# A graph kernel's message stage: the products of values and softmax weights go from VectorE to GpSimd

## The chip, the cores and the metric

The kernel runs on one core of a Trainium2 chip. The metric is the device time of one execution in microseconds (us), here the median of three runs. The profile is of one further execution.

## The reference

Four graph networks run one after the other on the same graph of 3125 nodes with 128 features and 50000 edges, sorted by destination. After each, the result is added to its input and normalised. The fourth is a graph transformer of two layers, and only the last step of its layer matters here. Cut to that:

```
m = vT[src, :, etype]                     # E x 8 heads x 16: the values of each edge
att = edge_softmax(a, dst, n)             # E x 8: a weight for each edge and head
msg = (m * att[:, :, None]).reshape(-1, H * HS)
hag = jax.ops.segment_sum(msg, dst, num_segments=n)
h = jax.nn.silu(typed_linear(hag, ntype, Wa))
```

All of it is float32.

## The kernel before

The edges lie in 416 tiles (`STEPS`) of 128. Each tile belongs to one block of 128 destination nodes. A segment sum over a tile is a matmul: a one-hot matrix, 128 edges by 128 destinations of the block, is the stationary operand, the messages of the 128 edges are the moving one, and the result is added to the block's columns in PSUM (`accf`). Four tiles are a quad, of which there are 104 (`ALL_QUADS`), and four quads are a trip. The first of the 26 trips is written out, the other 25 are a hardware loop (`trips`, L78).

`message_phase` (L1584) runs once in each of the transformer's two layers, after the scores and their softmax, and with a barrier before and behind it. Its instructions stand in four queues, and each queue is executed in its order:

- SyncE loads the values of a quad (256 KB, L1593) into one of four slots of `vals`. From the second trip on it waits until the product that used the slot is made (L1592).
- VectorE runs the helper `onehots` (L330): for each quad a wait that TensorE has finished the quad two before (`quad_done`, L339, as the one-hots have two buffers), the one-hots of four tiles in one comparison (128x512, L341), which signals `onehot_ready`, and then `weigh` (L1599): a wait for the values (`ring_in`, L1600) and the product of the values with the weights, 128x512, into one of two buffers of `msgs` (L1602), which signals `mixed`. Both `msgs` and `vals` are parts of the tile `arena`.
- TensorE clears the banks (`fill_rows`, L386), then for each quad loads one register with four packed block numbers (`quad_blocks`, L368), unpacks them (L370), waits for `mixed` (L1616) and makes four matmuls (L1619). Each is a float32 matmul, which the trace shows as two passes with a weight load each, so eight passes in a quad. The last one signals `quad_done`. TensorE does not wait for `onehot_ready`: VectorE makes the one-hot before the product.
- GpSimd and ScalarE have nothing to do in the stage.

In other stages GpSimd gathers rows by indirect DMA and copies columns (L1243, L1246). The aggregation stages (L531 to L547) have a TensorE loop of the same form that waits for two semaphores at the start of a quad: `onehot_ready` (L537) and the gathered rows (L540).

Of the kernel before, what the change touches and what calls it, by code (L numbers as in the profile page):

```python
# [5 lines left out]
ALU = mybir.AluOpType  # L6
# [4 lines left out]
ds = bass.ds  # L11

P = 128
# [7 lines left out]
U = 16  # L21
HALF = U // 2
QUADS = U // 4
# [15 lines left out]
HEADS = 8  # L39
HS = H // HEADS  # L40
# [34 lines left out]
def trips(eng, body, n=TRIPS):  # L75

    body(0, True)
    with eng.Fori(1, n) as i:  # L78
        body(i, False)
# [7 lines left out]
def build(nc, A, out):  # L87
    ctx = ExitStack()
    with ctx:
# [3 lines left out]
        def signal(name):  # L93
            return Signal(ctx.enter_context(nc.semaphore(name)))
# [65 lines left out]
        onehot_ready = signal("onehot_ready")  # L160
        compared = signal("compared")
        quad_done = signal("quad_done")
# [4 lines left out]
        mixed = signal("mixed")  # L167
# [4 lines left out]
        ring_in = [signal(f"ring_in{u}") for u in range(HALF)]  # L172
# [158 lines left out]
        def onehots(dve, weight, after=None):  # L331


            def body(i, first):
                for q in range(QUADS):
                    n = i * QUADS + q
                    j = i * U + 4 * q
                    if not (first and q < 2):
                        dve.wait_ge(quad_done.sem, quad_done.at(n - 1))  # L339
                    o = onehot[:, 4 * (q % 2):4 * (q % 2) + 4, :]  # L340
                    is_dst = dve.tensor_tensor(o, iota_row[:, :].unsqueeze(1).to_broadcast([P, 4, P]),  # L341
                                               dl_s[:, ds(j, 4)].unsqueeze(2).to_broadcast([P, 4, P]), ALU.is_equal)
                    if weight is not None:
                        is_dst.then_inc(compared.sem, 1)
                        dve.wait_ge(compared.sem, compared.at(n + 1))
                        is_dst = dve.tensor_tensor(o, o, weight[:, ds(j, 4)].unsqueeze(2).to_broadcast([P, 4, P]), ALU.mult)  # L346
                    is_dst.then_inc(onehot_ready.sem, 1)
                    if after is not None:
                        after(i, q, first)
            trips(dve, body)  # L350
            if weight is not None:
                compared.base += ALL_QUADS
# [13 lines left out]
        def quad_blocks(pe, n):  # L366

            four = nc.values_load(blk4_i[0:1, ds(n, 1)], engines=(pe.engine,), min_val=0, max_val=32 ** 4 - 1,  # L368
                                  skip_runtime_bounds_check_because="block numbers by construction")
            return [nc.snap((four >> (5 * c)) & 31, engines=(pe.engine,), min_val=0, max_val=NB - 1) for c in range(4)]  # L370

        def quad_pass_over():
            onehot_ready.base += ALL_QUADS
            quad_done.base += ALL_QUADS
# [6 lines left out]
        def fill_rows(pe, row):  # L381

            for k in range(BANKS):
                a, b, blocks = span(k)
                if row is None:
                    pe.matmul(accf[:, a:b], ident[:, :], zeros[:, 0:b - a], start=True, stop=False, skip_group_check=True)  # L386
                else:
                    pe.matmul(accf[:, a:b].rearrange("p (b f) -> p b f", f=H), ones[0:1, :],
                              row.unsqueeze(1).to_broadcast([1, len(blocks), H]), start=True, stop=False, skip_group_check=True)
# [576 lines left out]
        if STAGE >= 4:  # L966
# [13 lines left out]
            score = arena[:, 3200:3200 + STEPS * HEADS].rearrange("p (s h) -> p s h", h=HEADS)  # L980
# [19 lines left out]
            vals = arena[:, 7600:7600 + U * H].rearrange("p (r f) -> p r f", r=U)  # L1000
            msgs = arena[:, 9648:9648 + HALF * H].rearrange("p (r f) -> p r f", r=HALF)
# [582 lines left out]
            def message_phase():  # L1584

                with nc.Block() as block:
                    @block.sync
                    def _(sp):
                        def body(i, first):
                            for q in range(QUADS):  # L1590
                                if not first:
                                    sp.wait_ge(mixed.sem, mixed.at(i * QUADS + q - 3))  # L1592
                                sp.dma_start(vals[:, 4 * q:4 * q + 4, :],  # L1593
                                             values[ds(i * U + 4 * q, 4), :, :].rearrange("a e f -> e a f")).then_inc(ring_in[q].sem, 16)
                        trips(sp, body)

                    @block.vector
                    def _(dve):
                        def weigh(i, q, first):  # L1599
                            dve.wait_ge(ring_in[q].sem, ring_in[q].at(16 * (i + 1)))  # L1600
                            r = 4 * (q % 2)
                            dve.tensor_tensor(msgs[:, r:r + 4, :].rearrange("p s (h o) -> p (s h) o", o=HS),  # L1602
                                              vals[:, 4 * q:4 * q + 4, :].rearrange("p s (h o) -> p (s h) o", o=HS),
                                              score[:, ds(i * U + 4 * q, 4), :].rearrange("p s h -> p (s h)").unsqueeze(2).to_broadcast([P, 4 * HEADS, HS]),
                                              ALU.mult).then_inc(mixed.sem, 1)
                        onehots(dve, None, weigh)

                    @block.tensor
                    def _(pe):
                        fill_rows(pe, None)  # L1610

                        def body(i, first):
                            for q in range(QUADS):
                                blocks = quad_blocks(pe, i * QUADS + q)

                                pe.wait_ge(mixed.sem, mixed.at(i * QUADS + q + 1))  # L1616
                                for c, b in enumerate(blocks):
                                    o = onehot[:, 4 * (q % 2) + c, :]
                                    mm = pe.matmul(accf[:, ds(b * P, P)], o, msgs[:, 4 * (q % 2) + c, :],  # L1619
                                                   start=False, stop=False, skip_group_check=True)  # L1620
                                mm.then_inc(quad_done.sem, 1)
                        trips(pe, body)
                quad_pass_over()
                mixed.base += ALL_QUADS
                for s in ring_in[0:QUADS]:
                    s.base += 16 * TRIPS
# [138 lines left out]
```

## Time and profile before

| | |
|---|---|
| median of three runs | 7607.94 us (7606.06 to 7610.19) |
| the profiled execution | 7653.93 us |
| its span in the profile | 7652.2 us |
| TensorE busy, of the span | 4183.2 us (55%) |
| VectorE busy | 2372.6 us (31%) |
| GpSimd busy | 3561.7 us (47%) |
| the two message stages | 205.1 us each |

In the profile PE is TensorE's matmuls, PEld its weight loads, DVE is VectorE, ACT is ScalarE, POOL is GpSimd, SP is SyncE. A q behind an engine (PEldq) means its instruction queue: register, branch and semaphore instructions, which are not counted as busy. What ended an engine's idle time stands behind an arrow; "issue" means that the profile shows nothing that it waited for. PEclk is the granted clock of TensorE, where 1.0 is full speed.

### The profile page before, as it was taken

What the parts mean: (1) busy time and instruction counts of PE and PEld (TensorE: products, weight loads), DVE (VectorE), ACT (ScalarE), POOL (GpSimd) and SP (SyncE); (2) the same over time, 40 slices, a digit from 0 to 9 for tenths busy, and PEclk for the clock granted to TensorE, in tenths of its full rate; (3) what the DMA queues carried; (4) which work ended last, traced back from release to release, by engine and by line L of the source; (5) the groups of instructions that cost most, each with busy time, mean ns of one, the idle gap of its engine ahead of it and who ended that gap; (6) DMA issues with size and microseconds to landing.
All of it is one profiled execution on the core that took longest, in us unless ns stands there. A gap on an engine that the chain in (4) does not pass through costs nothing. (4 is left out here: it accounts for less than half of the span.)

```text
span 7652.2 us, 76944 instructions
## 1 busy us (share of the span) xinstructions
PE 4183.2 (55%) x15969; PEld 3034.6 (40%) x15970; DVE 2372.6 (31%) x3036; ACT 928.1 (12%) x1558; POOL 3561.7 (47%) x3650
## 2 busy tenths in 40 slices
PE   3566577667646666345443269544353299444352
PEld 2565445445435554233332134333242144333242
DVE  5222322322232223111111333233562233333753
ACT  0000222222211111000000012100000022000001
POOL 2675566366626663665676210466302201666111
PEclk8555676766765556556655589756586699656685
DMA  1111333233313332112211257544232367444241
GB/s 41 45 45 38 80 98 98 71 92 98 99 46 87 88 87 100 46 45 80 68 46 46 74 196 306 190 132 131 80 112 81 108 276 287 130 132 130 62 118 45
DMA packets 619686, 791.03 MB, mean 103 GB/s; under 512 B 89114, under 2 KB 508944, under 8 KB 594008
## 3 DMA queue, kind: packets, MB, share of 16 engines
q1 hardware_dynamic: 491800, 497.65, 19.4%
q0 software_dynamic: 127808, 292.52, 14.3%
q8 instruction: 27, 0.44, 0.0%
q14 instruction: 51, 0.42, 0.0%
HBM read 433.80 MB, written 356.02 MB: 103 GB/s over the span
## 5 line engine op out<-in xcount | busy, mean ns | idle before, releaser
L363 POOL DMA_INDIRECT G<-table,idx_s x3328 | 3329.2, 1000 | 2200.6 <-issue 934.9
L544 PE MATMUL ps<-G,onehot 128*128 128x128 f32 x4160 | 1169.0, 415 | 685.5 <-issue 506.2
L341 DVE TENSOR_TENSOR onehot<-iota_row,dl_s 128x512 f32<-128x512 f32 x1040 | 716.8, 690 | 1879.2 <-remote 1028.3
L544 PEld LDWEIGHTS ps<-G,onehot 128*128 128x128 f32 x4160 | 886.5, 286 | 905.8 <-issue 901.6
L1402 PE MATMUL ps<-arena 128*128 x1664 | 394.6, 395 | 505.0 <-issue 460.7
L1402 PEld LDWEIGHTS ps<-arena 128*128 128x128 f32 x1664 | 327.9, 283 | 581.3 <-issue 580.1
L1351 DVE TENSOR_TENSOR arena<-G,ps 128x512 f32<-128x512 f32 x208 | 142.7, 686 | 868.6 <-remote 533.6
L1262 PE MATMUL ps<-arena,G 128*128 128x512 f32 x800 | 379.1, 596 | 35.1 <-DVE arena L1294 35.1
L1305 DVE COPY arena<-ps 128x1024 f32<-128x1024 f32 x200 | 244.9, 1225 | 448.2 <-PE ps L1270 448.2
L1270 PE MATMUL ps<-arena,G 128*128 128x512 f32 x800 | 375.9, 592 | 0.0
L714 DVE TENSOR_TENSOR arena<-arena 128x256 f32<-128x256 f32 x208 | 88.6, 426 | 882.6 <-issue 529.8
L1097 POOL DMA_INDIRECT sorted_x<-Hn,pos_i x50 | 48.0, 961 | 653.6 <-POOLq L1652 639.0
L1619 PE MATMUL ps<-arena,onehot 128*128 128x128 f32 x1664 | 263.2, 310 | 135.3 <-issue 119.3
L635 PE MATMUL ps<-arena 128*128 128x256 f32 x416 | 204.8, 586 | 239.7 <-ACT arena L683 152.6
L859 PEld LDWEIGHTS ps<-ones,onehot 128*128 128x128 f32 x832 | 221.9, 327 | 265.6 <-issue 265.5
L543 PEld LDWEIGHTS ps<-ones,onehot 128*128 128x128 f32 x832 | 223.4, 328 | 252.0 <-issue 251.8
L859 PE MATMUL ps<-ones,onehot 128*128 128x1 f32 x832 | 191.7, 300 | 238.3 <-issue 127.7
L861 PE MATMUL ps<-onehot,arena 128*128 128x128 f32 x832 | 320.8, 489 | 0.0
L543 PE MATMUL ps<-ones,onehot 128*128 128x1 f32 x832 | 182.4, 289 | 240.5 <-DVE onehot L346 217.5
L1391 PE MATMUL ps<-ident,onehot 128*128 128x128 f32 x832 | 197.0, 383 | 197.0 <-issue 128.7
L1243 POOL COPY G<-HF 128x128 f32 (+1 forms) x50 | 14.8, 295 | 611.8 <-PE ps L1262 598.0
L1619 PEld LDWEIGHTS ps<-arena,onehot 128*128 128x128 f32 x1664 | 226.9, 212 | 171.4 <-issue 169.9
(287 smaller groups left out, 4715.0 us busy)
## 6 DMA issues: line engine op xcount, KB each, us to landing
table<-arena SPq DMA_DIRECT2D x200, 1024.0 KB
G<-table,idx_s POOLq DMA_INDIRECT x3328
values<-G SPq DMA_DIRECT2D x208, 256.0 KB
arena<-values SPq DMA_DIRECT2D x208, 256.0 KB
arena<-edge_times SPq DMA_DIRECT2D x208, 128.0 KB
edge_part<-arena SPq DMA_DIRECT2D x208, 128.0 KB
arena<-edge_part SPq DMA_DIRECT2D x416, 64.0 KB
table<-arena SPq DMA_DIRECT2D x50, 512.0 KB
```

Source lines behind the costliest of these rows:

```text
L341: is_dst = dve.tensor_tensor(o, iota_row[:, :].unsqueeze(1).to_broadcast([P, 4, P]), dl_s[:, ds(j, 4)].unsqueeze(2).to_broadcast([P, 4, P] ...
L363: pool.indirect_dma_start(G[:, j % U, 0:width], None, tab, bass.IndirectOffsetOnAxis(ap=idx_s[:, j:j + 1], axis=0)).then_inc(gathered[j % ...
L543: pe.matmul(misc[:, ds(b, 1)], o, ones[:, 0:1], start=False, stop=False, skip_group_check=True)
L544: mm = pe.matmul(accf[:, ds(b * P, P)], o, G[:, u, 0:H], start=False, stop=False, skip_group_check=True)
L635: pe.matmul(self.half_b, self.We2, self.hid[:, r, :], start=True, stop=True, skip_group_check=True).then_inc(turned.sem, 1)
L859: pe.matmul(misc[:, ds(b, 1)], o, ones[:, 0:1], start=False, stop=False, skip_group_check=True)
L861: mm = pe.matmul(accf[:, ds(b * P, P)], relu_h[:, u % HALF, :], o, start=False, stop=False, skip_group_check=True)
L1262: mm = pe.matmul(ps[:, s + c, :], node_cols[:, 0, :], block_k[:, 8 * q + 4 * c:8 * q + 4 * c + 4, :].rearrange("p t c -> p (t c)"), start= ...
L1270: mm = pe.matmul(ps[:, s + 2 + c, :], node_cols[:, 1, :], block_v[:, 8 * q + 4 * c:8 * q + 4 * c + 4, :].rearrange("p t c -> p (t c)"), st ...
L1305: dve.tensor_copy(rows32[:, q, :, H:2 * H], ps[:, 4 * (q % 2) + 2:4 * (q % 2) + 4, :].rearrange("p a (t f) -> p (a t) f", f=H)).then_inc(c ...
L1402: mm = pe.matmul(ps[:, 4 + q, c * P:(c + 1) * P], onehotT[:, q % 2, c * P:(c + 1) * P], Qn_flat[:, ds(b * P, P)], start=True, stop=True)
L1619: mm = pe.matmul(accf[:, ds(b * P, P)], o, msgs[:, 4 * (q % 2) + c, :], start=False, stop=False, skip_group_check=True)
```

## The change

VectorE keeps only the one-hots. GpSimd gets a program in the stage: for each quad it waits until TensorE has finished the quad two before, then for the values, and makes the product. TensorE waits for `onehot_ready` and for `mixed`, since the two now come from different engines. SyncE's program is as before.

```diff
                     @block.vector
                     def _(dve):
-                        def weigh(i, q, first):
-                            dve.wait_ge(ring_in[q].sem, ring_in[q].at(16 * (i + 1)))
-                            r = 4 * (q % 2)
-                            dve.tensor_tensor(msgs[:, r:r + 4, :].rearrange("p s (h o) -> p (s h) o", o=HS),
-                                              vals[:, 4 * q:4 * q + 4, :].rearrange("p s (h o) -> p (s h) o", o=HS),
-                                              score[:, ds(i * U + 4 * q, 4), :].rearrange("p s h -> p (s h)").unsqueeze(2).to_broadcast([P, 4 * HEADS, HS]),
-                                              ALU.mult).then_inc(mixed.sem, 1)
-                        onehots(dve, None, weigh)
+                        onehots(dve, None)
+
+                    @block.gpsimd
+                    def _(pool):
+                        def body(i, first):
+                            for q in range(QUADS):
+                                if not (first and q < 2):
+                                    pool.wait_ge(quad_done.sem, quad_done.at(i * QUADS + q - 1))
+                                pool.wait_ge(ring_in[q].sem, ring_in[q].at(16 * (i + 1)))
+                                r = 4 * (q % 2)
+                                pool.tensor_tensor(msgs[:, r:r + 4, :].rearrange("p s (h o) -> p (s h) o", o=HS),
+                                                   vals[:, 4 * q:4 * q + 4, :].rearrange("p s (h o) -> p (s h) o", o=HS),
+                                                   score[:, ds(i * U + 4 * q, 4), :].rearrange("p s h -> p (s h)").unsqueeze(2).to_broadcast([P, 4 * HEADS, HS]),
+                                                   ALU.mult).then_inc(mixed.sem, 1)
+                        trips(pool, body)
 
                     @block.tensor
                     def _(pe):
@@ -1613,6 +1620,7 @@
                             for q in range(QUADS):
                                 blocks = quad_blocks(pe, i * QUADS + q)
 
+                                pe.wait_ge(onehot_ready.sem, onehot_ready.at(i * QUADS + q + 1))
                                 pe.wait_ge(mixed.sem, mixed.at(i * QUADS + q + 1))
                                 for c, b in enumerate(blocks):
```

## Rows read from the trace of the kernel before

**Rows 1.** The page: busy us of each engine, share of the span.
```profile
PE 4183.2 (55%) x15969; PEld 3034.6 (40%) x15970; DVE 2372.6 (31%) x3036; ACT 928.1 (12%) x1558; POOL 3561.7 (47%) x3650
```

**Rows 2.** First message stage: length, PE, PEld, DVE, ACT, POOL busy, PEclk, DMA.
```profile
5584.20:5789.30 205.10, 136.87 (x846) 115.69 (x846) 133.67 (x208) 0.01 (x1) 0.00 (x0) 0.93 0.46 133
```

**Rows 3.** Timeline of a quiet trip: start us, length, engine, line.
```profile
5766.76 1.15 PE L1619 MATMUL ps<-arena,onehot 128*128 128x128 f32 x8 [1.09 <-issue]
5768.60 1.15 PE L1619 MATMUL ps<-arena,onehot 128*128 128x128 f32 x8 [0.68 <-issue]
5769.90 0.69 DVE L341 TENSOR_TENSOR onehot<-iota_row,dl_s 128x512 f32<-128x512 f32 x1 [0.54 <-PE ps L1619]
5770.43 1.15 PE L1619 MATMUL ps<-arena,onehot 128*128 128x128 f32 x8 [0.68 <-issue]
5770.51 0.68 DVE L1602 TENSOR_TENSOR arena<-arena 128x512 f32<-128x512 f32 x1
5772.25 1.15 PE L1619 MATMUL ps<-arena,onehot 128*128 128x128 f32 x8 [0.67 <-issue]
5774.56 0.71 PE L1619 MATMUL ps<-arena,onehot 128*128 128x128 f32 x4 [1.15 <-issue]
```

**Rows 4.** Lines L368, L370, L78 in TensorE's queue, first stage; ns min/median/max.
```profile
L368 PEldq TENSOR_LOAD <-blk_i x104: 296/301/331, 5584.3 to 5786.5; - x104
L370 PEldq ALU_OP  x416: 32/32/36, 5584.7 to 5787.4; - x139
L370 PEldq FUSED_REGOPS  x412: 40/58/68, 5584.8 to 5787.5; - x138
L78 PEldq COMPARE_BRANCH  x25: 76/208/218, 5602.1 to 5788.3; - x25
```

**Rows 5.** The matmul line L1619, whole span, with its waits.
```profile
L1619 PEldq FUSED_REGOPS  x832: 46/49/52, 5587.6 to 7422.6; - x167
  issue: 289.1, 333
  DVE arena L1602: 15.6, 19
```

**Rows 6.** The product line L1602, whole span.
```profile
L1602 DVE TENSOR_TENSOR arena<-arena x208: 680/684/693, 5586.9 to 7420.6; 128x512 f32<-128x512 f32 x104
```

**Rows 7.** Timeline where the clock is low.
```profile
5743.43 4.82 PE L1619 MATMUL ps<-arena,onehot 128*128 128x128 f32 x24 [1.12 <-issue]
5745.53 0.69 DVE L341 TENSOR_TENSOR onehot<-iota_row,dl_s 128x512 f32<-128x512 f32 x1 [1.78 <-PE ps L1619]
5748.92 1.15 PE L1619 MATMUL ps<-arena,onehot 128*128 128x128 f32 x8 [0.67 <-DVE arena L1602]
```

**Rows 8.** The wait line L540 of the aggregation stages, TensorE's queue.
```profile
L540 PEldq EVENT_SEMAPHORE  x395: 2/51/711, 130.0 to 4253.4; - x198
L540 PEldq FUSED_REGOPS  x75: 4/52/707, 160.0 to 4232.1; - x75
```

**Rows 9.** GpSimd's copies, line view.
```profile
L1246 POOL COPY G<-Hn x50: 295/296/301, 4482.7 to 6464.6; 128x128 f32 x48, 128x128 f32<-128x128 f32 x2
L1193 POOL COPY arena<-arena x2: 2848/2848/2849, 4472.8 to 6107.7; 128x3200 f32<-128x3200 f32 x2
```

**Rows 10.** Timeline at 4278, and VectorE's same operation at L488.
```profile
4278.06 2.85 POOL L1633 COPY Lx<-Xn 128x3200 f32<-128x3200 f32 x1 [28.69 <-ACTq L1630]
4278.07 3.28 DVE L1639 SCALAR_TENSOR_TENSOR arena<-src_s,t_s 128x416 f32<-128x416 f32 x1 [0.53 <-PEq L429]
L488 DVE SCALAR_TENSOR_TENSOR arena<-src_s,t_s x2: 591/592/592, 2933.9 to 3596.4; 128x416 f32<-128x416 f32 x2
```

**Rows 11.** Timeline at the start of the first message stage.
```profile
5584.20 14.79 SPq L1593 DMA_DIRECT2D arena<-values  x11
5586.85 0.69 DVE L1602 TENSOR_TENSOR arena<-arena 128x512 f32<-128x512 f32 x1 [1.92 <-DMA arena<-values]
5589.69 1.95 PE L1619 MATMUL ps<-arena,onehot 128*128 128x128 f32 x16
```

## The prediction

> **What bounds the kernel now.** I read the page first. The span is 7652.2 us and no engine is near full: TensorE is busy 55% of it, GpSimd 47%, VectorE 31% [rows 1]. That average says nothing of this change, which touches one stage, run twice: the message stage of the graph transformer. The stretches view has a row for each of the two runs, of which one is shown and the other is like it within 0.3%: 205.1 us each, 410.2 us together, 5.4% of the span. In them VectorE works 134 us, TensorE 137 us, GpSimd nothing at all [rows 2]. So no engine's arithmetic fills the stage, and the question is what sets the pace of a quad (four tiles, 104 quads in each run).
>
> The timeline of a quiet piece answers it [rows 3]. TensorE starts a quad at 5768.60, 5770.43 and 5772.25: 1.83 us each. Its eight passes take 1.15, then it idles 0.68, "issue", which names no releaser. Once in four quads the gap is 1.15. From 5766.76 to 5774.56, one trip of four quads, it is 7.80 us, or 1.95 a quad. VectorE starts the one-hot at 5769.90, that is 0.15 after the passes of 5768.60 end (5769.75), and the product at 5770.51; this is for the quad after the next (two buffers), so its end at 5771.19 is 1.06 us before TensorE uses it at 5772.25. The product is not what TensorE waits for.
>
> The line views of TensorE's own queue say what fills the gap [rows 4]. A quad needs: the load of the packed block numbers (one record of 0.30), four ALU_OP and four FUSED_REGOPS to unpack them (L370; 416 and 412 for 104 quads), a FUSED_REGOPS ahead of the load, and four more at the matmuls (832 in 208 quads, in [rows 5]). That is 14 steps in 1.83 us, through one in-order sequencer. Without the load's 0.30 it leaves 1.53 for 13 steps, 0.12 a step, though a record itself takes only 0.03 to 0.06. In the quad that begins a trip, three loop steps (L78) stand where one did; the gap is 0.47 longer (1.15 against 0.68), of which the branch's record is 0.21. The stage's pace is therefore TensorE's instruction stream. The waits view of the matmul line agrees: 289.1 us "issue" against 15.6 us put down to VectorE's product, in 19 places [rows 5].
>
> **The change, part by part.** *Removed from VectorE:* 208 products of 0.684 us [rows 6], with their waits. They lie beside TensorE's stream and the last of them is ready early, so I cost this at nothing. What it could return is the 15.6 us of 19 gaps [rows 5]. But such a gap is as long as an ordinary one: the one at 5748.92 is 0.67, put down to the product, where "issue" gaps are 0.68 [rows 3, 7]. On average the 19 are 0.82, so 19 x 0.14 = 2.7 us could come back at the most. I take 0.
>
> *Added to TensorE:* one more wait in each quad, 208 in all. Before, the wait for the product covered the one-hot too, as VectorE made it first; its wait is carried by the first address step. In the aggregation stages, where TensorE waits for two semaphores at the start of a quad, the first of them is a record of its own at L540, EVENT_SEMAPHORE or FUSED_REGOPS, of median 51 and 52 ns [rows 8]. So I expect one more step in the stream that sets the pace. Its price lies between the bare record, 0.05 (nothing, if it should fit into a gap that I don't see, but an in-order stream leaves none), and the mean step, 0.12. The mean includes long ones (the branch of memory and register steps), so I take 0.105: 208 x 0.105 = **+22 us**. The ends are +10 and +25. Behind this wait stand the eight weight loads and passes of the quad, and behind those the release of both buffers; everything in the stage shifts with it.
>
> *Added to GpSimd:* 208 products of 128x512 from two SBUF operands. No such operation is in the trace. The nearest rows are its copies, one input: 0.295 us for 128 elements, 2.848 for 3200 [rows 9]. That is 0.83 ns an element and 0.19 fixed, so 0.61 us for 512, the least it can be. If it reads its two inputs in turn, 1.04. If reads and the write all come in turn, 1.47. I take 1.25, between the last two, as the product must at least read twice what a copy reads. Rough bounds for the sum are 1.04 and 1.47.
>
> *Contention.* The one-hot and the product are now released together, by the same quad's passes. The trace has one case of such a pair. At 4278.06 GpSimd begins a copy of 2.85 us; 0.01 us later VectorE begins an operation with two SBUF inputs that takes 3.28 us, while the same operation on the same shape takes 0.592 elsewhere, and GpSimd's copy isn't slowed [rows 10]. VectorE stood still for 2.69 of the copy's 2.85. So they exclude each other, and the later one waits. The Trainium skill ("SBUF — State Buffer", Who interferes with whom) says this for a VectorE instruction with two SBUF inputs against a GpSimd one that reads SBUF; the trace agrees in its one case. By that rule the one-hot would always fall on one side of the product; without it they would overlap and nothing would be added.
>
> VectorE needs 0.15 from release to start, and GpSimd has two waits to pass before its instruction, so I let the one-hot go first: 0.15, then 0.61 (the spacing of VectorE's instructions, 5769.90 to 5770.51 [rows 3]), then 1.25, then some 0.2 until TensorE starts: 2.2 us after the release. TensorE's own stream gives 5772.25 - 5769.75 = 2.50 today and 2.50 + 2 x 0.105 = 2.71 with the new wait. So it is hidden with 0.5 to spare. Throughput: 0.61 + 1.25 + 0.1 for the two hand-overs = 1.96 a quad, against 1.95 + 0.105 = 2.05. Hidden too, by 0.1 only.
>
> Where the clock is low it isn't hidden. The granted clock is 0.93 over the stage [rows 2]: taking 1.2 against 2.4 GHz, 14% of it, some 29 quads. There TensorE starts at 5743.43 and releases VectorE only at 5745.53 - 0.15 = 5745.38, so 1.95 after its start instead of 1.15 [rows 7]. Two quads on is 3.66 + 0.21 = 3.87 after the start, 1.92 after the release; the chain needs 2.2. That is 0.28 late per two quads, 29 x 0.14 = 4 us; trips' long quads take a part of it back: **+3 us**.
>
> *The queues.* SyncE loads the values four quads ahead and waits for the product of the quad whose slot it refills. The product ends 0.6 us later than now (2.0 against 1.4 after the release), and three quads are 6 us; a load takes 2.65 us from issue to use (the first quad's: issued at 5584.20, product at 5586.85 [rows 11]). Hidden. At the stage's start TensorE clears its banks and starts the first quad at 5589.69; the second product would be made by 5586.85 + 2 x 1.25 = 5589.35 [rows 11]. Hidden. GpSimd's next work, after the stage, starts when the stage ends.
>
> **Sum.** The profiled execution took 7653.93 us (span 7652.2), 0.6% over the median of 7607.94. Its sum is 7653.93 + 22 + 3 = 7679; on the median, 7607.94 + 25 = **7633 us**, 0.33% slower.
>
> **Rivals.**
> *GpSimd sets the pace.* If the product is 1.47 and shares nothing with the one-hot, a quad is 0.61 + 1.47 + 0.1 = 2.18, 0.13 over 2.05: 208 x 0.13 = 27 us more, 7660. If the hand-overs cost the full 0.15 each and the one-hot its 0.69, it is 2.46, 85 us more, 7718, the far end. For it: the margin of my forecast is 0.1 us in a quad, and GpSimd's price is not in the trace. Against it: 0.14 of the copy's record didn't hold VectorE up, so records overlap at their ends. The Trainium skill ("GPSIMD Engine Reference", Performance versus the Vector engine) gives 4497 ns for a two-input addition of 2048 elements; no row here shows one. With the copies' fixed part that is an estimate of 1.27 us for 512, by which the sum would stay at 7633.
>
> *The wait costs nothing or half.* If the step is only its record, 208 x 0.05 = 10 us, 7618 with nothing added for the slow pieces; if it is swallowed, 7608. Against it: the 0.68 gap is itself made of nothing but such steps, each of which costs twice its record.
>
> *Faster.* The product leaves VectorE, which then has its one-hot ready at once, and the 15.6 us put down to the product in 19 gaps come back in full: 7592. It decides if these gaps were truly waits and the new wait is hidden under the load of the block numbers. Against it: their length is the length of any gap, and the first condition returns 2.7 us at most.
>
> **How the numbers follow.** Forecast (7620 to 7645) 0.60; GpSimd at the pace (7645 to 7718) 0.25; cheap or swallowed wait (7604 to 7620) 0.11; faster 0.04. The range leaves out the fastest case, half of the cheap one and the far end of the slow one: 7614 to 7675. A change of 0.2% is 15 us, about what a measurement of this kernel can tell. Slower by more: all of the first two but its low corner, 0.84. Within it 0.13. Faster by more 0.03.
>
> **What would show it.** In the profile after, the wait step appears in TensorE's queue at its line, 104 times a stage, and a quiet trip grows from 7.80 to 8.2 us with the gaps still "issue". Each stage takes 205.1 + 12 = 217 us. GpSimd has 208 products of about 1.25 us, or records up to 1.9 where the one-hot holds it up, and some one-hots of VectorE are far longer than 0.69. I am wrong if the TensorE gaps are put down to GpSimd in most quads (then the product is the pace), or if a quiet trip stays at 7.80 (then the wait is free).

## The result, and the profile after

Ten runs of each kernel, side by side: 7630.2 us median after (7624.29 to 7634.59), 7609.25 us before (7601.94 to 7615.32). The ratio is 1.0028, its 95% interval 1.0018 to 1.0038: 21 us slower, where 25 were forecast (7633). The profiled execution took 7634.59 us, close to its median, while that of the kernel before (7653.93) was 45 us above its own. So the two spans must not be subtracted; the message stages can be.

The stretches view of the changed kernel, its two message stages (length, then PE, PEld, DVE, ACT, POOL busy, PEclk, DMA share, GB/s):

```profile
5541.60:5758.40 216.80, 147.24 (x846) 124.50 (x846) 75.42 (x104) 0.00 (x0) 155.73 (x104) 0.88 0.43 126
7184.60:7401.70 217.10, 146.68 (x846) 124.01 (x846) 74.64 (x104) 0.00 (x0) 155.70 (x104) 0.88 0.43 126
```

Against 205.1 us each [rows 2] that is 11.7 and 12.0 longer, 23.7 together: the whole change of time, within what the runs can tell. VectorE's work has fallen from 134 to 75 us and nothing came of it.

The timeline of one quiet trip after, the answer to [rows 3]:

```profile
5641.45 0.69 DVE L341 TENSOR_TENSOR onehot<-iota_row,dl_s 128x512 f32<-128x512 f32 x1 [1.24 <-PE ps L1627]
5641.60 1.45 POOL L1609 TENSOR_TENSOR arena<-arena 128x512 f32<-128x512 f32 x1 [0.48 <-PE ps L1627]
...
5644.48 1.15 PE L1627 MATMUL ps<-arena,onehot 128*128 128x128 f32 x8 [1.27 <-DVE onehot L341]
5646.41 1.15 PE L1627 MATMUL ps<-arena,onehot 128*128 128x128 f32 x8 [0.78 <-issue]
5648.34 1.15 PE L1627 MATMUL ps<-arena,onehot 128*128 128x128 f32 x8 [0.77 <-issue]
5650.25 1.15 PE L1627 MATMUL ps<-arena,onehot 128*128 128x128 f32 x8 [0.75 <-issue]
```

The next quad starts at 5652.67, so the trip takes 8.19 us; it was 7.80. The passes take 1.15 as before, and each gap has grown by 0.08 to 0.12. TensorE's queue has what makes it so, the new wait as a record of its own, 104 times a stage. It is only 36 ns long in 200 of the 208 cases (the forecast expected 51 or 52), but the next step of the queue starts 0.097 us after it (median in the trace):

```profile
L1624 PEldq ALU_OP  x200: 36/36/36, 5553.7 to 7400.1; - x100
L1624 PEldq EVENT_SEMAPHORE  x8: 51/51/51, 5545.4 to 7194.7; - x8
```

GpSimd's product, and what waited for it (first line: ns min/median/max):

```profile
L1609 POOL TENSOR_TENSOR arena<-arena x208: 1055/1502/1562, 5544.3 to 7398.2; 128x512 f32<-128x512 f32 x104
...
  PE ps L1627: 18.4, 29
```

The shortest is 1.055 us; with a one-hot beside it, it is 1.45 to 1.56.

### The profile page after: what moved, and what is told of

Its sections match the earlier page's. It is cut to its first block and busy times, and to the rows that moved or that the text cites. A ratio compares the mean times of both kernels' runs of the same rounds, so it can differ in the third digit from the quotient of the medians.

```text
span 7632.8 us, 77558 instructions
## 1 busy us (share of the span) xinstructions
PE 4239.0 (56%) x15969; PEld 3069.8 (40%) x15970; DVE 2256.0 (30%) x2828; ACT 928.5 (12%) x1558; POOL 3869.6 (51%) x3858
## 5 line engine op out<-in xcount | busy, mean ns | idle before, releaser
L1609 POOL TENSOR_TENSOR arena<-arena 128x512 f32<-128x512 f32 x208 | 311.4, 1502 | 343.4 <-DMA arena<-values 230.5
L1627 PE MATMUL ps<-arena,onehot 128*128 128x128 f32 x1664 | 283.0, 324 | 139.5 <-issue 64.7
L1627 PEld LDWEIGHTS ps<-arena,onehot 128*128 128x128 f32 x1664 | 243.5, 225 | 178.8 <-issue 177.1
L543 PE MATMUL ps<-ones,onehot 128*128 128x1 f32 x832 | 190.0, 298 | 215.9 <-DVE onehot L346 189.3
```

The lines of the kernel that those rows point to most:

```text
L543: pe.matmul(misc[:, ds(b, 1)], o, ones[:, 0:1], start=False, stop=False, skip_group_check=True)
L1609: pool.tensor_tensor(msgs[:, r:r + 4, :].rearrange("p s (h o) -> p (s h) o", o=HS), vals[:, 4 * q:4 * q + 4, :].rearrange("p s (h o) -> p ...
```

## The experiments

They ran on two chips: the unrolled loop, alone and with the short unpacking, and the changed kernel run again on chip 3, all others on chip 5. Both execute the kernel before in 7056 to 7064 us, against 7609 in the result above: the stages that gather rows are faster there (in the changed kernel GpSimd is idle before its gathers for 1612 us there, for 2157 above). The message stage isn't: the changed kernel run there (`e8_changed_again`) has 217.1 and 216.6 us. So ratios are taken against the kernel before on the same chip, and stage lengths are compared directly, with 205.1 for the kernel before, whose stage was not profiled there. The whole times bear this out: they change by 16 us where the two stages say 21.7 (one wait more), and by 39, -28, -18 and -40 where they say 42, -24, -16.5 and -39 (two waits, short unpacking, unrolled loop, both). Each stage length is from one profiled execution.

### One wait more, and nothing else

```diff
+                                pe.wait_ge(onehot_ready.sem, onehot_ready.at(i * QUADS + q + 1))
                                 pe.wait_ge(mixed.sem, mixed.at(i * QUADS + q + 1))
```

> The kernel before, with the new wait of TensorE for the one-hots alone; VectorE still makes the products. If the cost is a step in TensorE's instruction stream: 0.10 us in each of 208 quads, 20 us, some 7629 us, and each message stage 215.5 us instead of 205.1. If the cost is GpSimd's slower product or the two engines getting in each other's way: no change, 205.1 us a stage, some 7609 us.

```profile
5082.90:5298.80 215.90, 140.50 (x846) 118.86 (x846) 134.07 (x208) 0.00 (x0) 0.00 (x0) 0.91 0.44 126
6625.70:6841.70 216.00, 141.59 (x846) 119.86 (x846) 134.11 (x208) 0.00 (x0) 0.00 (x0) 0.91 0.44 126
```

7074.69 us against 7058.56, ratio 1.0025 (1.0014 to 1.0035). Each stage is 10.8 to 10.9 longer, 21.7 together or 0.104 us a quad, for a wait that is always met when the next one is: VectorE still makes the one-hot first and the product 0.61 us behind it. This one line gives 21.7 of the 23.7 us of the change. GpSimd has no work here. The whole kernel is 16 us longer (10 to 25), which the 21.7 fit.

### Two waits more

```diff
+                                pe.wait_ge(onehot_ready.sem, onehot_ready.at(i * QUADS + q + 1))
+                                pe.wait_ge(ring_in[q].sem, ring_in[q].at(16 * (i + 1)))
                                 pe.wait_ge(mixed.sem, mixed.at(i * QUADS + q + 1))
```

> The kernel before, with two more waits in TensorE that are always met: for the one-hots, and for the load of the values. If each wait is a step of 0.10 us in the stream that sets the pace: twice the one-wait cost, 226 us a stage, some 7650 us. If the first wait only takes up a gap or replaces another step: clearly less than twice, under 220 us a stage.

226.2 us in both stages, 21.1 over the kernel before, 1.95 times what one wait costs; 7097.5 us, ratio 1.0056 (1.0040 to 1.0071). The second wait costs nearly what the first does (10.3 against 10.8 us a stage): there is no gap that takes a step up.

### GpSimd makes the products, TensorE has one wait

```diff
-                                if not (first and q < 2):
-                                    pool.wait_ge(quad_done.sem, quad_done.at(i * QUADS + q - 1))
+                                pool.wait_ge(onehot_ready.sem, onehot_ready.at(i * QUADS + q + 1))
                                 pool.wait_ge(ring_in[q].sem, ring_in[q].at(16 * (i + 1)))
...
-                                pe.wait_ge(onehot_ready.sem, onehot_ready.at(i * QUADS + q + 1))
                                 pe.wait_ge(mixed.sem, mixed.at(i * QUADS + q + 1))
```

> The changed kernel without the new wait in TensorE: GpSimd waits for the one-hots of its quad in place of TensorE's passes, so that the signal of the product covers both, as before. If the cost is the step in TensorE's stream: it is gone, 205 to 208 us a stage, 7609 to 7615 us (0 to 3 us a stage stay for the slow-clock pieces and the start, as the chain one-hot, product is longer). If the cost is GpSimd's product: it stays or grows, as the two now always run one after the other, 217 us a stage or more, 7630 us or more.

213.7 and 211.1 us, 7068.75 us, ratio 1.0015 (1.0006 to 1.0024). Neither expectation holds. The step is gone, but 8.6 and 6.0 us a stage are back as another wait. Here is a piece where the clock is low:

```profile
5169.23 5.21 PE L1625 MATMUL ps<-arena,onehot 128*128 128x128 f32 x24 [1.19 <-POOL arena L1608]
...
5173.28 0.69 DVE L341 TENSOR_TENSOR onehot<-iota_row,dl_s 128x512 f32<-128x512 f32 x1 [1.47 <-PE ps L1625]
5174.17 1.06 POOL L1608 TENSOR_TENSOR arena<-arena 128x512 f32<-128x512 f32 x1 [1.03 <-DVE onehot L341]
...
5175.38 1.15 PE L1625 MATMUL ps<-arena,onehot 128*128 128x128 f32 x8 [0.93 <-POOL arena L1608]
```

The chain behind a release is now one-hot, signal, product, signal: TensorE's passes end 0.15 before 5173.28, the product starts 0.89 after the one-hot, ends at 5175.23, and TensorE starts at 5175.38, 2.25 us after the release. Passes at the low clock release late, so three quads took 6.15 us, 2.05 each, where the stream needs 1.83. TensorE starts 0.15 us after a product's end when that is what it waited for. By these starts (within 0.2 us), 59 of the 208 quads waited for the product here, 22 in the changed kernel; the 59 come 7.8 and 5.4 us a stage later than the stream's pace, about the 8.6 and 6.0 that are to be explained. (The matmul line puts 125.8 us of idle time down to the product here, far more than these waits; why is told below.) The changed kernel avoids this chain by starting both at the release, and pays with the second wait.

### A shorter instruction stream on the kernel before

The message stage gets a helper of its own for the unpacking; cut to what it does otherwise:

```diff
-            return [nc.snap((four >> (5 * c)) & 31, ...) for c in range(4)]
+            parts = [four & 31, (four >> 5) & 31, (four >> 10) & 31, four >> 15]
+            return [nc.snap(p, ...) for p in parts]
```

> The kernel before, where in the message stage the first block number is unpacked without its shift and the last without its mask; everything else is as it was. If TensorE's instruction stream sets the pace: one and a half to two steps of 0.10 us less in each quad, 31 to 42 us less, 7567 to 7578 us, 185 to 190 us a stage. If something else (VectorE's two operations and their signals, or the passes) is right behind it: less than 15 us are saved, over 197 us a stage, with the gaps before the matmuls put down to VectorE.

192.9 and 193.0 us, 12.1 to 12.2 less a stage, 7030.7 us, ratio 0.9963 (0.9949 to 0.9977). The direction is as the first theory has it, the size is smaller than it said. The queue shows why: six records a quad instead of eight, but the last of the six is long, up to 145 ns, and in a quiet quad the next step starts 0.20 us after it instead of 0.10. So the two records less save 0.117 us a quad, 0.06 each:

```profile
L377 PEldq ALU_OP  x624: 32/32/36, 5083.4 to 6794.9; - x156
L377 PEldq FUSED_REGOPS  x624: 53/62/145, 5083.5 to 6795.0; - x156
```

### TensorE's loop unrolled, alone and with the short unpacking

```diff
-                        trips(pe, body)
+                        body(0, True)
+                        with pe.Fori(0, (TRIPS - 1) // 5) as o:
+                            for k in range(5):
+                                body(o * 5 + (k + 1), False)
```

> The kernel before, with TensorE's loop of 25 trips in the message stage written as 5 rounds of 5 trips; nothing else is changed. A trip's first quad is 0.42 us longer for its three loop steps. If TensorE's instruction stream sets the pace: 20 of the 25 loop ends go, 20 x 0.42 = 8.4 us a stage, 196.6 us, 17 us in all, ratio 0.9976, less what a longer program costs to fetch. If the longer quad is from elsewhere (the wait for values, VectorE's own loop): under 2 us a stage.

196.8 and 196.9 us a stage (196.6 expected), 7037.93 us, ratio 0.9974 (0.9965 to 0.9984).

> The short unpacking and the unrolled loop together, on the kernel before. If both only shorten TensorE's stream they add up: 192.9 - 8.4 = 184.5 us a stage, 41 us in all, ratio 0.994. If VectorE's chain (one-hot and product, 1.3 us of work a quad and the signals) comes up behind it: less, 188 us or more, with gaps put down to VectorE.

185.5 and 185.3 us, 7015.3 us, ratio 0.9939 (0.9926 to 0.9953). The two add up to within 1 us a stage. This is the version that beats both kernels, with VectorE still making the products and one wait in TensorE.

### The changed kernel again, and at the shorter stream

> The changed kernel once more, on the same chip as the experiments. Ratio 1.0025 to 1.0030 to the kernel before, 216.8 us a stage: 10.8 for the wait, about 1 for GpSimd. If this chip's other speed outside the stage changes the cost, the ratio is off that.

217.1 and 216.6 us, ratio 1.0032 (1.0020 to 1.0045). The result above was 1.0028; both agree within the interval.

The next kernel is the changed one with the short unpacking and the unrolled loop.

> The changed kernel (GpSimd makes the products, TensorE has the second wait) with the short unpacking and the unrolled loop. TensorE's stream then needs 1.73 + 0.10 = 1.83 us a quad. If one-hot and product one after the other need 0.5 + 1.06 + 0.1 = 1.7 us, they still stay behind it: 185.4 + 10.8 + 1 to 2 = 197 to 198 us a stage. If they need the 1.96 us of the forecast: they are the pace, 205 us a stage or more, with most gaps put down to GpSimd or VectorE.

195.1 and 194.9 us, 7045.84 us, ratio 0.9974 (0.9962 to 0.9985). That is 2 to 3 us less than even the lower expectation. Against the same kernel with VectorE's products it is 9.6 longer a stage, no more than the wait, and GpSimd adds nothing that can be seen. Quads start 1.80 us apart here (median within a trip), so even there GpSimd isn't the pace, and the 1.96 us of the forecast are refuted.

### GpSimd's product twice

The first of two equal products goes into a buffer that nobody reads.

> The changed kernel, with GpSimd making each product twice, first into a buffer that nobody reads, then as before. An unhindered product takes 1.056 us. If GpSimd and the one-hot exclude each other, as the longer records of the changed kernel say, a quad needs 2 x 1.06, about 0.5 for the one-hot that comes first, and 0.1 to 0.2 for starts: 2.7 to 2.8 us, and as the products are then the pace, stages of 285 to 300 us. If they overlap and the longer records only count waiting for something else: 2.2 to 2.3 us a quad, stages of 235 to 245 us. If TensorE's stream were still the pace: 217 us.

263.1 and 262.8 us, one run of 7183.73 us. The first and the second product:

```profile
5151.56 1.50 POOL L1609 TENSOR_TENSOR arena<-arena 128x512 f32<-128x512 f32 x1
...
5153.02 1.05 POOL L1613 TENSOR_TENSOR arena<-arena 128x512 f32<-128x512 f32 x1
5153.04 1.58 DVE L341 TENSOR_TENSOR onehot<-iota_row,dl_s 128x512 f32<-128x512 f32 x1 [0.90 <-PE ps L1631]
5154.04 1.50 POOL L1609 TENSOR_TENSOR arena<-arena 128x512 f32<-128x512 f32 x1
```

A quad takes 5154.04 - 5151.56 = 2.48 us, between the two expectations. GpSimd never pauses, so that is its own need: two products spaced 1.02 apart and 0.44 lost once. The last two lines show the exclusion from the other side: a one-hot that starts 0.02 after a product takes 1.58 instead of 0.69, and the next product, begun at 5154.04 before it ends, is the long one. So they do exclude each other, but for 0.44 us a quad, less than the 0.5 that I put in, and less than the one-hot's own 0.61, so there is no sign of time lost at the hand-over.

## Why the prediction was right

*TensorE's stream is the pace.* Shown from four sides: one wait more costs 0.104 us a quad, two cost 1.95 times that, two records less and fewer loop ends give 12 and 8 us a stage back, and these add up to within 1 us.

*The new wait: 0.105 us a quad, +22 us.* Measured alone: 0.104, +21.7. The rival in which it costs nothing or its record alone has fallen: the record is 0.036 us and the step costs nearly three times that.

*Removing the product from VectorE: nothing.* Right. The wait alone, with VectorE still doing both, gives 215.9 and 216.0; with VectorE relieved it is 216.8 and 217.1. That is the net of both, but there was nothing to give back: in the kernel before, 9 of the 208 quads start within 0.2 us of the product's end, and none of them comes more than 0.01 us later than the stream's pace. So the 15.6 us put down to the product [rows 5] were no time lost, and the faster rival has fallen.

*GpSimd and contention: +3 us.* Measured 2: the difference between the changed kernel and the one with the wait alone, 0.9 and 1.1 us a stage. It has two parts that can be seen. At the start TensorE's third quad waits for a product made after the first passes:

```profile
5548.26 3.03 POOL L1609 TENSOR_TENSOR arena<-arena 128x512 f32<-128x512 f32 x2 [1.90 <-PE ps L1627]
...
5550.07 1.15 PE L1627 MATMUL ps<-arena,onehot 128*128 128x128 f32 x8 [1.00 <-POOL arena L1609]
```

The third quad starts 2.95 us after the first (5547.12), 2.65 in the kernel with the wait alone: 0.3 us a stage. I hadn't costed that wait; my text looked only at the first two quads. The other part is the one forecast, where the clock is low:

```profile
5564.23 3.69 PE L1627 MATMUL ps<-arena,onehot 128*128 128x128 f32 x16 [0.78 <-issue]
...
5566.50 1.56 POOL L1609 TENSOR_TENSOR arena<-arena 128x512 f32<-128x512 f32 x1 [1.29 <-PE ps L1627]
...
5568.20 1.15 PE L1627 MATMUL ps<-arena,onehot 128*128 128x128 f32 x8 [0.29 <-POOL arena L1609]
```

Passes released this product at 5566.30, it ends at 5568.06, and TensorE starts 1.90 us after the release, two quads and 3.97 us after 5564.23, where two quiet quads take 3.86. The 22 quads that wait in this way all follow passes at the low clock and come at most 0.12 us late each, 0.4 and 0.7 us a stage. About 0.3 us of the 2 stay unexplained.

So the mechanism was there, but that 3 came so near to 2 is in part luck. The wait is shorter than forecast (1.90 us after the release, not 2.2), more of the stage runs at the low clock (0.88 after, where I took the 0.93 of before), and the start wasn't costed.

*The sizes in it were off on the careful side.* The product is 1.055 us, not 1.25. From the 2048-element figure of the Trainium skill ("GPSIMD Engine Reference", Performance versus the Vector engine) my estimate was 1.27. For that size it says VectorE is about twice as fast with two inputs; here, with 512 elements and one input repeated over 16 of them, 1.055 against 0.684 us is 1.54 times. The one-hot holds the product up for 0.44, not 0.61. One-hot and product together need 2.48 - 1.02 = 1.46 us a quad, not 1.96. That the stage stayed on TensorE's stream was therefore no near thing: the rival "GpSimd sets the pace", to which I gave 0.25, was much further off than its 0.1 us of margin said: it would have needed over 0.5 us more a quad.

*What would show it.* The trip grew to 8.19 (8.2 forecast), the stage to 216.8 and 217.1 (217). GpSimd's records are up to 1.56 us, not 1.9, and the longest one-hot of VectorE is 1.26. But "the gaps still issue" was only half right:

```profile
L1627 PE MATMUL ps<-arena,onehot 128*128 128x128 f32 x1664 | 283.0, 324 | 139.5 <-issue 64.7 <-DVE onehot L341 55.3 <-POOL arena L1609 18.4
```

and for the kernel with the wait alone:

```profile
L1620 PE MATMUL ps<-arena,onehot 128*128 128x128 f32 x1664 | 271.2, 315 | 149.2 <-issue 75.2 <-DVE onehot L341 64.0 <-DVE arena L1602 9.0
```

The 55.3 and 64.0 us are no real waits. In the kernel with the wait alone they can't be, since the product comes after the one-hot; in the changed kernel the one-hot had ended 1.4 us or more before TensorE's start in all 45 gaps. The gap before 5644.48 is put down to the one-hot, but its one-hot is the one that the passes of 5640.15 release: it began at 5641.45 and ended at 5642.14, over 2 us before the gap's end. A wait that stands in a gap draws the gap to its semaphore, met or not; only the end of the instruction that signals it tells.

## What to carry to other kernels

When the gaps between an engine's instructions are "issue" and filled with its queue's own records, count those records: relieving another engine gives nothing, and each further step is paid. The price isn't the length of the record and differs from step to step: here 0.10 us for a wait, 0.41 for a loop end of three steps, 0.06 for each of two unpacking records saved. Splitting work that one semaphore covered over two engines adds a wait for its consumer; chaining the second engine behind the first removes that wait but makes the release-to-ready chain longer, which costs where passes are slow. Shorten the stream first (here 40 us from a few lines), then see what comes up behind it.

## What the runs showed of the hardware that I had not expected

The granted clock of the message stage went, roughly, with its pace. It is 0.93 before, 0.91 with one wait more, 0.88 in the changed kernel (0.87 and 0.89 when run again), 0.85 and 0.82 with two waits more, 0.64 with the product twice; with the loop unrolled it is 0.97 and 0.98, and with the shorter unpacking 1.00, that is 2.4 GHz throughout:

```profile
5082.90:5275.80 192.90, 125.03 (x846) 103.09 (x846) 134.44 (x208) 0.00 (x0) 0.00 (x0) 1.00 0.49 141
```

Pace alone doesn't settle it: with both shortenings the clock is 0.99 at 185.5 us, and GpSimd with one wait has 0.88 at 213.7 us, less than the 0.91 of one wait more at 215.9. In the kernel before the low clock costs nothing: the three quads from 5743.43 to 5748.92 [rows 7] take 5.49 us, 1.83 each, as in the quiet trip. In the changed kernel it costs the 0.4 and 0.7 us a stage found above.
